# Six conditioning jobs over thirteen instead of fifteen attention rounds: three parts in rounds 5, 9, 10 and 11, none in 13 to 15

## What is computed

```python
def _bi_wkv(r, k, v, w, u, time_emb):      # k = v = fside, r = x
    tf = sigmoid(sum(time_emb, axis=-1))
    decay = exp(-exp(w)) * (0.5 + 0.5 * tf)
    ek = exp(minimum(k, 30.0)); ekv = ek * v
    nf, df = scan forward, nb, db = scan backward of a = a * decay + (ekv, ek)
    euk = exp(minimum(u + k, 30.0))
    num = nf + nb - ekv + euk * v
    den = df + db - ek + euk
    return sigmoid(r) * (num / maximum(den, 1e-08)) * (0.8 + 0.2 * tf)

x = x + attention(cond(x, fside, fside, w, u, cond_512), Wq, Wk, Wv, Wg, Wd, Wo)
x = x + experts(cond(x, fside, fside, w2, u2, cond_512), gate_weight, gate_up_weights, down_weights)
```

## Time and profile before

| | us |
|---|---|
| median of 3 runs | 524.43 (522.4 to 524.53) |
| the profiled execution | 527.21 |
| its span | 525.4 |
| PE busy in the span | 456.2 (87%) |
| DVE, ACT, POOL busy | 345.7, 310.5, 213.5 |
| attention rounds 5 to 15 | 134.7 to 299.0 |

### The profile page before, as it was taken

How to read it: one execution, slowest core, us unless ns; L and a number is a source line. 1 busy time by engine, 2 the same in 40 slices (tenths; PEclk the granted TensorE clock), 3 DMA queues, 4 the chain that set the end, 5 groups by cost and what they waited for, 6 DMA issues and landing times.

```text
span 525.4 us, 10372 instructions
## 1 busy us (share of the span) xinstructions
PE 456.2 (87%) x3073; PEld 343.8 (65%) x3073; DVE 345.7 (66%) x1204; ACT 310.5 (59%) x854; POOL 213.5 (41%) x224
## 2 busy tenths in 40 slices
PE   4487889999999889998998957868999999999476
PEld 1266677787777768786886643446777777777222
DVE  4948769559668678739859883835567777674043
ACT  4366687689585787968798670113436656666200
POOL 0323402006012365111357877403666666666600
PEclk9889899999999999999999977979999999999879
DMA  7931494000030011200029997499855555560297
GB/s 268 418 138 36 87 193 108 20 1 1 0 83 0 30 65 71 78 5 2 21 82 380 406 408 282 116 300 310 276 143 161 157 148 156 166 166 18 55 404 293
DMA packets 47318, 79.49 MB, mean 151 GB/s; under 512 B 8266, under 2 KB 31127, under 8 KB 46880
## 3 DMA queue, kind: packets, MB, share of 16 engines
q1 hardware_dynamic: 36544, 55.08, 33.4%
q0 software_dynamic: 7680, 16.93, 8.9%
q10 hardware_dynamic: 3040, 6.82, 4.0%
HBM read 56.54 MB, written 26.44 MB: 158 GB/s over the span
## 4 chain that ended last, share of the span: by engine, by line
PE 52%; DVE 15%; ACT 14%; DMA 9%; issue 5%; POOL 3%; SPq 2%; DVEq 0%; POOLq 0%; ACTq 0%
PE ps L1698 11%; PE ps L1400 8%; PE ps L1719 7%; PE ps L1525 6%; ACT lg L696 4%; DVE lg L1042 3%; ACT lg L639 3%; DMA pairs<-pair_rows 3%; PE ps L1448 2%; PE ps L1396 2%; POOL slot_rows L618 2%; PE ps L1397 2%; PE ps L1398 2%; DMA xrow<-slot_rows 2%; DMA pair_rows<-eout,dest 2%
## 5 line engine op out<-in xcount | busy, mean ns | idle before, releaser
L625 POOL DMA_INDIRECT pair_rows<-eout,dest x93 | 91.9, 988 | 62.4 <-ACT eout L639 40.4
L696 ACT ACTIVATE lg<-lg,mneg 128x128 f32<-128x128 f32 (+1 forms) x128 | 56.4, 443 | 26.1 <-DVE mneg L1042 26.1
L1698 PE MATMUL ps<-wts,xg 128*64 (+1 forms) x512 | 70.2, 339 | 1.2 <-DVE xg L1319 1.1
L546 POOL DMA_INDIRECT slot_rows<-rows,pair_slot x48 | 48.4, 1009 | 34.6 <-issue 23.6
L1698 PEld LDWEIGHTS ps<-wts,xg 128*64 128x64 f32 x512 | 52.3, 141 | 13.2 <-issue 5.7
L1525 PE MATMUL ps<-oT,wo_sb 128*128 128x256 f32 x240 | 54.4, 380 | 0.0
L1319 DVE COPY xg<-ps 128x512 f32<-128x512 f32 (+1 forms) x50 | 33.4, 667 | 31.0 <-PE ps L1400 28.8
L1525 PEld LDWEIGHTS ps<-oT,wo_sb 128*128 128x128 f32 x240 | 44.6, 190 | 6.2 <-ACT oT L639 0.7
L838 ACT ACTIVATE sact<-ps 128x192 f32<-128x192 f32 (+1 forms) x50 | 16.2, 325 | 51.5 <-PE ps L1698 49.1
L639 ACT ACTIVATE lg<-lg,rinv 128x128 f32<-128x128 f32 (+1 forms) x128 | 45.9, 449 | 0.8 <-DVE rinv L1050 0.8
L1719 PE MATMUL ps<-wts,aT 96*64 96x256 f32 (+1 forms) x256 | 46.0, 379 | 0.4 <-ACT aT L639 0.4
(11 more groups left out here) (237 smaller groups left out, 1199.8 us busy)
## 6 DMA issues: line engine op xcount, KB each, us to landing
wts<-in_experts_dram SPq DMA_DIRECT2D x22, 640.0 KB, 14.0
xrow<-slot_rows SPq DMA_DIRECT2D x188, 65.0 KB
pairs<-pair_rows SPq DMA_DIRECT2D x16, 512.0 KB, 9.6
wts<-in_experts_dram ACTq DMA_DIRECT2D x10, 640.0 KB, 7.9
slot_rows<-zero SPq DMA_DIRECT2D x1, 4160.0 KB, 24.3
wT<-in_wq_t_dram SPq DMA_DIRECT2D x4, 512.0 KB, 6.2
wq_raw<-in_wq_l_dram SPq DMA_DIRECT2D x1, 2048.0 KB, 14.7
wo_sb<-in_wo_l_dram SPq DMA_DIRECT2D x1, 2048.0 KB, 20.6
```

The lines of the kernel that those rows point to most:

```text
L546: nc.gpsimd.indirect_dma_start(out=slot_d, out_offset=bass.IndirectOffsetOnAxis(ap=pair_slot[:, t, k:k + 1], axis=0), in_=r[:, k, :], in_o ...
L625: nc.gpsimd.indirect_dma_start(out=pair_d, out_offset=bass.IndirectOffsetOnAxis(ap=dest[:, d:d + 1], axis=0), in_=out_rows(d), in_offset=N ...
L696: ins = nc.scalar.activation(t, t, ACT.Exp, bias=mneg[:, u % 2, c:c + 1], scale=-1.0, accum_out=rsum[:, u % 2, c:c + 1])
L1698: ins = nc.tensor.matmul(ps[h * R:(h + 1) * R, 2 + u % 2, k * I2:(k + 1) * I2], xg[u % len(xg)][:, k, cc, h * R:(h + 1) * R], moving, star ...
```

## The change

`round_parts` deals out three parts in rounds 5, 9, 10 and 11 (one early, two late) and two in the others up to round 12; the last three rounds have none. The split send of block 4 goes, since no part 2 is left in round 13.

```diff
+        THICK = (5, 9, 10, 11)
+
         def round_parts(u):
-
-            return round_jobs[2 * u:2 * u + 1], round_jobs[2 * u + 1:2 * u + 2]
+            first = 2 * u + sum(1 for r in THICK if r < u)
+            return round_jobs[first:first + 1], round_jobs[first + 1:first + (3 if u in THICK else 2)]
...
                         if part == 2:
-                            for t in sent_in(u):
-                                if t == TB * QUICK:
-                                    number_rows(t)
-                                    send_rows(t, range(TOPK // 2))
                             cond_sums((c, jb))
...
                 for t in sent_in(u):
-                    if t == TB * QUICK:
-                        send_rows(t, range(TOPK // 2, TOPK))
-                    else:
-                        number_rows(t)
-                        if t == LAST[0] - 1:
-                            number_last_rows(LAST[1])
-                        send_rows(t, range(TOPK))
+                    number_rows(t)
+                    if t == LAST[0] - 1:
+                        number_last_rows(LAST[1])
+                    send_rows(t, range(TOPK))
```

## The result

The changed kernel takes 549.7 us (median of 4 runs, 548.43 to 550.22), the kernel before 524.48 (4 runs): 1.048 times as long, 95% interval 1.044 to 1.051. It is slower by 25.2 us; the forecast was 546.0. The profiled execution took 549.52 and has a span of 547.7. The kernel before had 525.4, which is only 22.3 less, because that one execution lost 2.3 us in a part that is the same in both: 0.8 ahead of the first logits (granted clock between 20 and 40 us 0.74, and 0.83 in this one) and 1.5 between those of units 1 and 2 (granted clock between 52 and 72 us 0.91, and 0.95). The first logits of unit 7 start at 150.54 before and at 148.25 after. So I measure everything from there. "Unit u" is what the prediction calls round u when it speaks of scores or logits: they are made two rounds ahead, unit 8 in round 6.

A forecast was written before the change was run, and what follows sets the result against it. No engine's load bounds the kernel; what stands in queues ahead of instructions other engines wait for does. Terms 3.7 + 5.7 + 8.6 + 3.6 = 21.6 us on the median give 546.0 us; own range 538 to 551, widened to 533 to 554.

The forecast's parts named there:

- A: Rounds 5 to 8: part 2 ahead of the picks makes PE wait; costs 3.7 us, bounds 0.5 to 5.
- B: Rounds 9 and 10: parts 0 and 1 ahead of route_h(1) delay PE's route logits; costs 5.7 us, bounds 3.3 to 7.0.
- C: Rounds 10 to 15: late parts delay picks, the addition to xT and logits; costs 8.6 us, bounds 6 to 9.9.
- the ring: Each round's loop: PE scores, DVE logits, ACT exponentials, PE transposes; queue order ahead of awaited instructions counts, not engine load.
- Clock: Behind PE's stalls in rounds 6 and 10: lower clock costs 1.8 us each, 3.6 together; bounds 0 to 5.4.
- Partly absorbed: Rival, 533 us, chance 0.10: only the delay of rounds 9 and 10 and one clock drop (5.7 + 1.8) stay.
- Faster: Rival, 517 us, chance 0.04: some 7.5 us leave the chain, including waits in round 7, and routing results aren't missed.
- Heavier: Rival, 552 us, chance 0.11: POOL holds DVE's products in both places, third clock drop, rounds 10 to 15 at upper bound.

The follow-up runs named there:

- e8: Changed kernel, with ACT's two exponentials of an early part 0 in rounds 7 and 11 moved behind its copies; 544.1 us beside 523.4 for the kernel before.
- e6: Changed kernel, with round 9's third part moved to round 8; 549.0 us beside 523.4 for the kernel before.
- e3: Changed kernel, with DVE's picks of rounds 5 and 10 and route_h of round 9 ahead of the late parts; 537.2 us beside 523.8 before.
- e9: Changed kernel without round 11's third part (three parts in rounds 5, 9 and 10 only); 545.0 us beside 523.9 for the kernel before.
- e1: Changed kernel, with round 5's third part moved to round 8; 546.1 us beside 523.8 for the kernel before.
- e4: Changed kernel, with POOL's sums of round 5 waiting for DVE's picks and its product of round 9 for route_h; 544.0 us beside 523.8 before.
- e10: Changed kernel, with 6 and 7 throwaway PE matmuls during its waits in rounds 6 and 10; 544.1 us beside 523.9 for the kernel before.
- e5: Changed kernel, with 14 throwaway PE matmuls ahead of each wait in rounds 6 and 10, overrunning both; 555.3 us beside 523.4 before.

## Why the prediction was right, and which terms were off

The direction, the places and the mechanism of A and B were right; the sum was 21.6 and the loss is 25.2 (24.6 between the two traces). A and B were each 1.9 too small, and C came out 0.8 smaller than forecast, but only with 3.0 of clock in it that I had not put there. That part of the agreement is luck.

**A: 3.7 expected, and 1.8 of clock; measured 7.4.** Its structure is right. Part 2 ahead of the picks makes PE wait (6.72, forecast 5.8), then the ring gets 0.3 back between units 8 and 9 (7.7 to 7.3; I had 4.1 to 3.7), because a wait for part 0 (2.28) takes the place of the one for hf. e8 shows that this new wait costs 3.3. Two sizes were off. I had seen POOL hold a weight but hadn't asked what POOL does behind part 2: its sums start right there and hold the picks for 1.7. Only 1.0 of that is new, and with the 4.1 of part 2 it makes the 5.0, since in the kernel before POOL's masks (L519, 156.73 to 157.95) held the same picks for 0.7:

```profile
157.48 0.81 DVE L1078 TENSOR_TENSOR before<-before,picked 128x64 f32<-128x64 f32 x2
```

And the clock cost 2.6, not 1.8: it was low for 5.4 us of work instead of the 2.8 to 4 that I had read off. A's upper bound, 5, was given to another hold, in round 7. That one showed too (DVE's product at 194.30 took 1.55 instead of 0.69) and cost no more than 0.3 of unit 10.

**B: 5.7 expected, and 1.8 of clock; measured 9.4.** DVE's wait for ACT was 2.48 (forecast 2.5), its wait for the clock 1.8 (1.8). The term that was too small is part 1: 3.15 in the sum, 4.9 in the trace, since POOL's product and its masks run beside the four scans. I had weighed this hold for the wrong instruction: DVE's product started 0.05 ahead of POOL's and was not held, the scans behind it were. I had put it into the range (1.28) rather than into the sum. What e6 adds: the wait for ACT could not be taken out by moving part 0 early in the round, since ACT then waited for it.

**C: 8.6 expected; measured 7.8.** About the right size, in part by luck. Picks 1.4 later: right (PE's wait 2.44 instead of 1.00). Unit 13 3.8 later: 3.5, and for the reason given, ACT's wait for part 0 in round 11 (4.53). e3 shows that it alone makes the 3.5. e8 takes it away and wins only 0.4, because PE's own way, 1.4 late by the picks and then at the low clock, is nearly as long: two causes side by side, of which either is enough. Two late parts in round 11: right, and with the weights the largest piece (6.4, e9), though only one weight was held and not two (2.73 for the eight, forecast 3.7 with 2.0 of hold). Their effect is not where I said: not the route logits of round 13 released by DVE, but a stage earlier, PE's wait of 5.06 for ql in front of unit 14's scores. From 283.47 to 307 the chain of what ended last is PE alone, and round 13's route logits stand in it, at 292.12, without a wait.

What I had not seen is what follows. From unit 14 (+26.7) to unit 15 (+22.2) 4.5 come back, although the clock is low for 6.0 us of that way. From the end of PE's wait for ql to unit 15's logits it takes 18.2 us in the changed kernel, 17.2 in e1, 17.0 in e4 and 16.8 in e8, with the clock low for 6.0, 4.0, 3.4 and 3.1: again half of the low time, which leaves 15.2 to 15.3 in each. So 3.0 of C is this fourth drop. Up to the last projection (315.47, 292.54 before) 3.0 are lost again, as ACT waits 1.36 for DVE's rinv, which stands behind a block's weights. The same stretch costs 3.0 to 3.3 in e1, e3, e4, e8 and e10, so what unit 15 loses or wins is carried on. Behind the last projection 0.6 come back. By this reckoning C would be 4.8 without the clock.

**Clock.** I had two drops and a third in the bound; there are four. The third, in round 11, costs nothing that shows: e1, e3, e4, e5 and e10 don't have it, and their unit 13 loses the same 3.5. The fourth, in round 12, costs the 3.0 above. The two that were forecast cost 2.6 and, against the kernel before, 1.8.

**Rivals.** "Partly absorbed" falls with A and C, which it had at under 1 each. "Faster" decided at PE's two waits: they grew to 6.7 and 7.4. "Heavier" had the right additions, holds in both new places and a third drop of the clock, with 552 against 549.7; what it lacked was that C would give something back. My own range, 538 to 551, is narrower than the bounds of the terms, which add up to 534 and 552. The profile counts 224 instructions on POOL in both kernels, so none was lost there. The stretch behind the last projection is 0.6 shorter than before, within the 1 us that I gave it.

## What to carry to other kernels

Work in small steps between two stages is free only if nothing that another engine waits for stands behind it in its queue: here 11.4 of 24.6 us went when the routing was put ahead of the same parts, and 6 us were to be had in the kernel before by moving two side jobs of ACT behind its copies. Look, in every queue, for a wait for a side product ahead of something that the ring needs. When a step is moved, list what its end releases on the other engines too (here POOL's sums and products), since that runs beside whatever now follows it, and a hold there is a term of the sum and not only of the range. When two waits lie side by side, taking one away says only how far behind it the other lies.

## What the runs showed of the hardware

- The granted clock fell at a different distance from the wait in each place: 1.9 us into the wait of round 6, 5.0 us into that of round 10, and in e3 and e10 only 1.4 and 1.5 us behind the end of waits of 2.98 and 1.39. So a shorter wait, or a filled one, may move the drop onto the work behind it instead of sparing it. In the four places of the changed kernel it was low for 3.4 to 6.0 us of PE's work, and each microsecond of that cost half a microsecond where PE was what the ring waited for, and nothing that shows in round 11, where it was not.
- DVE and POOL hold each other for whole instructions, scans included: 0.69 became 1.64 and 1.05, and POOL's own product 1.28 became 1.77. An instruction with one input was held as well: `picked`, 0.61 beside POOL's sum and 0.23 without it (e4).
- A load of ACT's table is not bound to the wait of the instruction that it is for: in round 12 of the changed kernel it ran at 276.09 for 1.28, and its sigmoid began at 278.97, when DVE's xT came.
